# Cross attention: the second exponentials and the low parts of a pair, made and waited for head by head

## What is computed

```python
    def _L0_xattn_ref(x, context, mask, gamma, ctx_gamma, Wq, Wkv, Wout, Wff1, Wff2):
        heads, dim_head = (16, 64)
        scale = dim_head ** (-0.5)
        xn = layer_norm(x, gamma)
        ctx = layer_norm(context, ctx_gamma)
        q = (xn @ Wq).reshape(b, n, heads, dim_head).transpose(0, 2, 1, 3) * scale
        kv = ctx @ Wkv
        k, v = (kv[..., :dim_head], kv[..., dim_head:])
        sim = jnp.einsum('bhid,bjd->bhij', q, k)
        sim = jnp.where((mask == 0)[:, None, None, :], -jnp.inf, sim)
        attn = jax.nn.softmax(sim, axis=-1)
        out = jnp.einsum('bhij,bjd->bhid', attn, v)
        out = out.transpose(0, 2, 1, 3).reshape(b, n, heads * dim_head)
        out = out @ Wout
        ...
```

## Time and profile before

| | us |
|---|---|
| median of 3 runs | 2379.47 |
| lowest and highest | 2375.77, 2381.38 |
| the profiled execution, its own time | 2383.35 |
| its span in the trace | 2381.6 |
| PE, PEld busy | 2107.6, 1587.9 |
| DVE, ACT, POOL busy | 1336.2, 672.7, 616.9 |
| cross attention, pair 0 to the last output | about 66 to 653 |

### The profile page before, as it was taken

One profiled execution on the slowest core, in us unless ns is written; L12 is line 12 of the kernel. 1 busy time (PEld: TensorE's weight loads), 2 busy tenths in 40 slices (PEclk: granted clock), 3 DMA queues, 4 the chain that ended last, 5 costly groups with the idle time before them and its releaser, 6 DMA issues. The chain is left out here.

```text
span 2381.6 us, 29531 instructions
## 1 busy us (share of the span) xinstructions
PE 2107.6 (88%) x11169; PEld 1587.9 (67%) x11169; DVE 1336.2 (56%) x2128; ACT 672.7 (28%) x1066; POOL 616.9 (26%) x553
## 2 busy tenths in 40 slices
PE   6999999999989999999999999998998444454898
PEld 5677777777677788888888888887873111121577
DVE  7766676656447777766776676666651000000387
ACT  2644564446433331112111211122421000000231
POOL 5444554445377941320032000000320000000010
PEclk9999999999999999999999999998997667687899
DMA  4223223322297669664966494434879999999767
GB/s 157 77 103 130 79 70 112 130 80 68 97 366 260 239 246 344 228 228 172 339 227 233 165 366 159 159 123 155 323 286 430 430 425 428 428 429 427 278 230 265
DMA packets 182379, 565.10 MB, mean 237 GB/s; under 512 B 15305, under 2 KB 98793, under 8 KB 152393
## 3 DMA queue, kind: packets, MB, share of 16 engines
q1 hardware_dynamic: 172936, 504.37, 56.4%
q10 hardware_dynamic: 9312, 58.99, 6.0%
HBM read 450.07 MB, written 113.25 MB: 237 GB/s over the span
## 5 line engine op out<-in xcount | busy, mean ns | idle before, releaser
L1447 PE MATMUL ff_down<-w,u 128*128 128x512 f32 x1536 | 362.4, 394 | 8.5 <-DVE ff_x L1720 8.3
L1387 PE MATMUL ff_up<-ff_t,w 128*128 128x512 f32 x1488 | 358.1, 389 | 3.9 <-ACT ff_gate L1520 3.9
L1447 PEld LDWEIGHTS ff_down<-w,u 128*128 128x128 f32 x1536 | 290.8, 190 | 73.7 <-DVE ff_x L1720 13.0
L1387 PEld LDWEIGHTS ff_up<-ff_t,w 128*128 128x128 f32 x1488 | 279.5, 188 | 62.3 <-issue 4.3
L1720 DVE SCALAR_TENSOR_TENSOR ff_x<-ff_down,gates,ff_x 128x512 f32<-128x512 f32 x256 | 191.1, 749 | 87.0 <-PE ff_down L1447 85.1
L2503 PE MATMUL e_down<-e_w,e_ug 128*32 128x512 f32 x480 | 74.6, 778 | 185.5 <-DMA e_w<-in_L_ffn_e_W 104.3
L1387 PE MATMUL ff_up<-ff_b,w 128*128 128x512 f32 x954 | 235.5, 391 | 0.0
L1387 PEld LDWEIGHTS ff_up<-ff_b,w 128*128 128x128 f32 x954 | 179.9, 189 | 37.5
L2503 PEld LDWEIGHTS e_down<-e_w,e_ug 128*32 128x32 f32 x480 | 18.5, 137 | 240.4 <-issue 130.6
L1512 ACT ACTIVATE ff_gate<-ff_gate 128x512 f32<-128x512 f32 x62 | 39.2, 633 | 406.6 <-DVE ff_gate L1696 406.6
L2611 DVE TENSOR_TENSOR e_u_rows<-e_turned,e_b1T 128x128 f32<-128x128 f32 x16 | 4.7, 292 | 266.2 <-PE e_turned L2494 266.2
(11 more groups left out here) (451 smaller groups left out, 4360.0 us busy)
## 6 DMA issues: line engine op xcount, KB each, us to landing
w<-ff_w_factors SPq DMA_DIRECT2D x48, 1792.0 KB, 7.6
e_wg<-in_L_ffn_e_Wg SPq DMA_DIRECT2D x15, 4096.0 KB, 33.7
e_w<-in_L_ffn_e_W SPq DMA_DIRECT2D x14, 4096.0 KB, 26.2
e_w<-in_L_ffn_e_W ACTq DMA_DIRECT2D x13, 4096.0 KB, 51.9
ff_w_factors<-w SPq DMA_DIRECT2D x15, 1792.0 KB, 7.2
w<-ff_w_parts SPq DMA_DIRECT2D x48, 512.0 KB, 5.4
ff_t<-ff_t_factors SPq DMA_DIRECT2D x16, 1024.0 KB, 15.0
e_w<-in_L_ffn_e_W SPq DMA_DIRECT2D x16, 1024.0 KB, 10.0
```

Source lines behind the costliest of these rows:

```text
L1387: last = nc.tensor.matmul(bank[:, :], a, m, start=start and c == 0, stop=stop and c == 5)
L1447: last = nc.tensor.matmul(DN[m % 2][:, :], a, w, start=c == 0, stop=c == 5)
```

## The change

The second exponentials of a pair become two instructions of 128x512, one for each head, and each raises `probs`. The subtraction on DVE becomes two as well: each waits for its head's exponentials, and each raises `low_probs`. PE waits for `low_probs` ahead of each of the two L635, not once ahead of both. The two other waits for `probs` count double. L758, which writes `prob_hi`, stays one instruction.

```diff
                     if b or i:
-                        pe.wait_ge(probs, b * HP + i)
+                        pe.wait_ge(probs, 2 * (b * HP + i))
...
-                    pe.wait_ge(low_probs, b * HP + i + 1)
                     for odd in range(2):
+                        pe.wait_ge(low_probs, 2 * (b * HP + i) + odd + 1)
                         last = nc.tensor.matmul(OB[:, odd, :], hi[:, cols[odd]], prob_lo[:, odd, :], start=False, stop=True)
                     last.then_inc(heads_out, 1)
...
                         if i == 0 and t == 0 and b < late:
-                            pe.wait_ge(probs, (b + 1) * HP)
+                            pe.wait_ge(probs, 2 * (b + 1) * HP)
...
                     nc.scalar.activation(two(prob_hi[:, :, :]), two(SC[:, :, :]), ACT.Exp, bias=bias).then_inc(hi_probs, 1)
-                    nc.scalar.activation(two(prob[:, :, :]), two(SC[:, :, :]), ACT.Exp, bias=bias).then_inc(probs, 1)
+                    for odd in range(2):
+                        nc.scalar.activation(prob[:, odd, :], SC[:, odd, :], ACT.Exp, bias=bias).then_inc(probs, 1)
...
                 def low_probs_of(b, i):
-                    dve.wait_ge(probs, b * HP + i + 1)
-                    nc.vector.tensor_tensor(two(prob_lo[:, :, :]), two(prob[:, :, :]), two(plain(prob_hi[:, :, :])), ALU.subtract).then_inc(low_probs, 1)
+                    for odd in range(2):
+                        dve.wait_ge(probs, 2 * (b * HP + i) + odd + 1)
+                        nc.vector.tensor_tensor(prob_lo[:, odd, :], prob[:, odd, :], plain(prob_hi[:, odd, :]), ALU.subtract).then_inc(low_probs, 1)
```

## The result

| | us |
|---|---|
| kernel before, median of 4 runs (2375.77 to 2384.48) | 2380.43 |
| changed kernel, median of 4 runs (2405.71 to 2414.20) | 2406.94 |
| ratio, 95% interval | 1.0113 (1.0097 to 1.0130) |
| profiled execution of the changed kernel, its span | 2414.20, 2412.4 |

The kernel became 26.5 us slower. The forecast was 7.3 us faster, and the range ended at 2377.0. The page of the changed kernel first: engine, busy us, share of the span, instructions; then the group of the halved subtraction (busy us, mean ns, idle time before it).

The account below looks back on a forecast made before the run. PE was taken to bound steady pairs at 5.99 us, leaving gains only where it stalls for `prob_lo`. Terms 2.8, 1.9, 1.8 and 0.75 made 7.3 us off the median 2379.5, giving 2372.2; range 2367.0 to 2377.0.

Parts of the forecast that it names:

- The step that failed: DVE's halves: POOL slowing both subtractions leaves the second head's low part 0.15 us earlier, within 0.15 to 0.34.
- ACT's halves: Second exponentials on ACT: 0.68 us per half, the second starting 0.58 us after the first.
- The 0.16 us more on ACT: Extra ACT time per pair of halves, claimed covered by L744's wait for PE's queries.
- DVE's halves: Subtractions of 0.69 us each, without overlap; low part 0.26 us earlier for the second head, 0.97 for the first.
- Steady pairs zero: Some 44 of 64 pairs: L635 already follows without a gap, PE's own 5.99 us stay, zero gain.
- the 44 quiet pairs: The steady pairs, 44 or so of 64, where PE has no gap and the forecast gain was zero.
- Last batch: Six pairs: period falls from 5.99 us to about 5.5, 0.47 us a pair, 2.8 us in all.
- Pair 3 and its like: Pair 3 of batches 1 to 5, 0.24 us each, plus four single pairs, 0.69 us: 1.9 us gain.
- batch ends: Seven batch ends: L966 and L597 start 0.26 us earlier each, 1.8 us gain.
- Batch 0, pair 4: Earlier statistics on DVE and earlier low part let PE's matmuls finish sooner: 0.75 us gain.
- the clock rival: Batch 0, pair 4: less PE idle keeps its clock full, another 3.1 us gain, 2369.1 us; chance 0.20.
- The slower rival: Wait between the two L635 breaks PE's stream, 0.11 to 0.28 us a pair, 2379.2 to 2390.1 us; chance 0.05.

Follow-up runs that it names:

- e6: Changed kernel with POOL's subtraction of oT_lo replaced by a memset to zero; 2379.71 us, ratio 0.9991.
- e2: Kernel before, with POOL taking up a pair's outputs only after DVE has made the next pair's low parts; 2385.58 us, ratio 1.0017.
- e1: Changed kernel, with POOL taking up a pair's outputs only after both DVE halves of the next pair; 2374.36 us, ratio 0.9965.
- e3: Changed kernel with only ACT's exponentials halved; DVE waits for both and subtracts once, PE waits once; 2388.24 us, ratio 1.0024.
- e8: e1 with one wait of PE ahead of both L635 instead of one per head; 2373.90 us, ratio 0.9974.
- e5: Changed kernel with one wait of PE for both low parts ahead of both L635; 2418.16 us, ratio 1.0143.
- e4: Changed kernel with only DVE's subtraction halved; ACT's second exponentials stay one instruction, PE waits per head; 2416.36 us, ratio 1.0159.
- e7: Changed kernel with POOL waiting for the next pair's low parts between its cast and its subtraction; 2377.86 us, ratio 0.9982.

## Why the prediction was wrong

**The step that failed** is the sentence "If POOL slows both subtractions as it does in pair 3 (1.48 instead of 1.23), 0.15". It read POOL's influence as a surcharge on DVE's duration, of 0.25 us at most, and so bounded the low part between 0.15 and 0.34 us earlier. Measured, it is 1.07 us later (2.92 against 1.85). The right question was not how much slower an instruction gets but which of the two starts first, and whether the cut gives the other one a turn. The rows for it were in the trace of before and I didn't look at them: L881 with a median of 2120 ns and a minimum of 1269 was waiting in most pairs, 0.20 us behind DVE's L974.

The Trainium skill states the rule, which I had not weighed. "SBUF — State Buffer", section "Who interferes with whom", says that a DVE instruction with two SBUF inputs contends with a GpSimd (POOL) instruction that reads SBUF and not with one that only writes it. Section "SBUF: two separate sides" of the same page says that whoever of the two starts first gets the shared ports for the whole instruction. The runs agree: 2.73 us with the reading subtraction, 1.64 with the writing memset (e6), and an uncut subtraction of 2.30 us in e2. By rows of before alone a rival could then have been priced: POOL's cast starts 0.06 us after `acc` (595.58 to 595.64), its subtraction 0.82 after it (596.40) and takes at least 1.27 (the minimum of L881), and a second half of up to 0.69 behind that ends at +2.8, against 2.92 measured.

Point by point:
- *ACT's halves:* right. 683 ns for a forecast of 0.68, with 0.57 us from start to start for 0.58. DVE's first half starts 0.19 us after `acc`, as worked out. The 0.16 us more on ACT stayed covered: where POOL keeps away, steady pairs have 5.99 us (e1).
- *DVE's halves:* 0.69 us each is right when free, but the second starts 0.61 behind the first and not 0.71, so the two take 1.29. The low part is then 0.37 us earlier (e1), more than the 0.26 of the sum. Under POOL, all of this is swept away.
- *Steady pairs zero:* right for a gain (5.99 in e1), wrong as a risk. I wrote that the second wait is met "long before". e3 shows that a low part 0.16 us later costs 0.15 us in nearly every pair: PE's own 5.99 and the loop's 5.99 lay on top of each other. So the 44 quiet pairs, which could give nothing, could lose much, and with them the outcome was one-sided.
- *Last batch:* the working holds where DVE is free. Forecast 5.50 to 5.52, e1 5.53; there the six pairs gave 2.5 us for a forecast of 2.8.
- *Pair 3 and its like, batch ends:* in e1 2.1 us for 1.9, and 2.7 for 1.8 (34.15 instead of 34.51 each, the low part being 0.37 and not 0.26 earlier). Pair 6 took 1.0 back, which was not forecast. The 1.48 us of pair 3 were rightly put down to POOL, but they weren't all that held the pair: e2, without POOL in the way, gained nothing there.
- *Batch 0, pair 4, and the clock:* in e1 the two periods from pair 3 on are 7.98 and 6.24 us, 8.98 and 8.92 before, so 3.7 us less for the forecast's 0.75 plus the rival's 3.1. The granted clock from 84 to 112 us was 1.00 in e1, 0.88 before and 0.89 in the changed kernel. The stream in e1 stood once, for 1.76 us, and not twice for 1.91 and 0.57; in the changed kernel it stood for 2.36 and 1.18 us. That looks like the clock rival, and e8, which stood for 1.76 us as well, has 1.00 too. But e2 stands against it as the whole reason.

PE in e2, then its row by stretch (us, PE, PEld, DVE, ACT and POOL busy, clock, DMA share, GB/s):

```profile
97.77 0.47 PE L631 MATMUL att_out<-prob_hi,v_hi 128*128 128x512 f32 x1 [1.91 <-DVE acc L983]
...
99.53 0.72 PE L635 MATMUL att_out<-prob_lo,v_hi 128*128 128x512 f32 x2 [0.59 <-DVE prob_lo L976]
```

```profile
84.00:112.00 28.00, 25.50 (x126) 18.24 (x124) 22.06 (x37) 18.06 (x27) 14.08 (x12) 1.00 0.00 1
```

It stood for 1.91 and 0.59 us, as the kernel before did, and its clock stayed full; the two periods are 8.88 and 6.08, 2.9 us less than before. So it isn't shown that less idle time is what keeps the clock, and some 2.9 us of e1's gain in its profile may belong to the execution and not to the halves.

Together e1 gives 10.2 us from pair 0 to pair 63 in its profile, and 8.6 between the medians: about what forecast and clock rival promise in sum. With the 2.9 us of the clock taken off the profile's figure, some 7.3 are left, the forecast's own size (an estimate from single profiles). The gain that was forecast exists; the changed kernel doesn't get it.

**The slower rival** had the right place and the wrong cause. It put the loss between the two L635, and that is where the matmul stands for 1.03 us. But it held that PE can't load behind a wait, at most 0.28 us a pair, and the wait turned out a small gain (e5, e8). What the matmul waits for is DVE, and DVE waits for POOL. With 0.05 for everything slower, the mistake in the chances is the same as in the sum: the only slow way I had thought of was one that a row already spoke against.

## What to carry to other kernels

Before an instruction is cut in two, look at who shares its memory access and is waiting beside it: an uncut instruction keeps a neighbour out for its whole length, and a cut gives the neighbour a turn in the middle. A neighbour's instruction that is much longer at the median than at its minimum is the sign of it. If the cut is worth it, order the neighbour behind it with a wait (here one wait on POOL turned 1.011 into 0.997), and check where the neighbour's postponed work lands. And ask of every quiet place not only what it can gain but how much slack it has against a loss.

## What the runs showed of the hardware

- DVE's subtraction with two SBUF operands and POOL's subtraction, addition or cast from SBUF don't run beside each other. The one that starts behind ends a fixed time after the first: POOL's 1.13 us after DVE's in the kernel before (597.43 to 598.56) and in e3 (610.47 to 611.60), DVE's half 0.55 after POOL's subtraction in the changed kernel and in e4 (639.71 to 640.26) and as much after the cast in e7 (609.28 to 609.83), DVE's uncut one 1.09 after L113 in e2 (266.39 to 267.48). That is its own duration less 0.14 to 0.16 us in each case, as if only its start were overlapped.
- A head start of 0.05 us decides it (e3), and so does one of 0.08 the other way (e2).
- POOL's normalisation L851, a tensor_scalar of 2.08 us from SBUF, is different: it holds DVE in its first part alone. A half that starts 0.51 us behind it takes 0.80 us (the first of the pair at 267.85), one 0.23 us behind it takes 1.07 (e7, at 186.18); both end 1.30 to 1.31 us after L851's start. A half that starts 0.70 us behind it takes its free 0.69 (e5, at 271.15). Nearer to its start the order isn't settled: in e2 the uncut subtraction begins 0.14 us behind L850, the same line there (at 253.19), takes its free 1.23, and L850 takes 3.15. The other way round L851 waits for DVE: begun during a half, it takes 2.51 us (at 250.09). By the Trainium skill's rule quoted above, L851 should hold DVE for its whole 2.08 us; here the traces decide. Why it lets DVE pass was not tried.
- DVE instructions with one SBUF input seem to be held too: in e2 the two tensor_scalar of 128x128, L920 and L923, took 0.50 and 0.47 us beside POOL instead of 0.22. L920 ends 0.08 us after POOL's subtraction. No run separates this.
- Two DVE halves of 0.69 us take 1.29 us together in e1, and so do those of the first pair of a batch in the changed kernel: the second starts 0.08 us before the first ends.

Open: whether e1's remaining collision in pair 6 (0.24 us in each of five batches) can be moved away, which was not tried, and what decides the clock that an execution is granted from 60 to 80 us and around pair 4 of batch 0.
